# A language-model layer on one core: Down tail on 128 rows, quantiser in two list steps, four sums on GpSimd, new lists

## What is computed

```python
emb = (w0[inputs] @ w1) * mask * 16.0                     # A: rows of 512, then 512 x 256
x = layernorm(emb)                                         # y, the residual of the block
h = layer_norm(x, ln1_g, ln1_b); hx = token_shift(h)
k, v, r = mixes of h and hx, each @ (256 x 256); r = sigmoid(r)
wkv = wkv_scan(k, v, time_decay, time_first)               # recurrence over time, per channel
x = x + (r * wkv) @ wo                                     # B
h = layer_norm(x, ln2_g, ln2_b); hx = token_shift(h)
kk = square(relu(mix(h, hx) @ cwk)); rr = sigmoid(mix(h, hx) @ cwr)
x = x + rr * (kk @ cwv)                                    # 256 -> 1024 -> 256
h1 = emb + x
xq = fp4(layernorm(h1))                                    # C
g = silu(xq @ fp4(w_gate).T) * (xq @ fp4(w_up).T)          # 256 -> 704
out = h1 + fp4(g) @ fp4(w_down).T                          # 704 -> 256
```

## Time and profile before

| | us |
|---|---|
| median of 3 runs | 775.6 (773.82 to 776.73) |
| span of the profiled execution | 772.5 |
| one period, 145.65 to 230.13 | 84.48 |
| PE busy over the span | 701.0 (91%) |
| DVE | 591.7 (77%) |
| ACT | 509.2 (66%) |
| POOL | 144.3 (19%) |
| mean granted TensorE clock | 0.964 |

### The profile page before, as it was taken

How to read it: one execution, slowest core, us unless ns; L and a number is a source line. 1 busy time by engine, 2 the same in 40 slices (tenths; PEclk the granted TensorE clock), 3 DMA queues, 4 the chain that set the end, 5 groups by cost and what they waited for, 6 DMA issues and landing times.

```text
span 772.5 us, 9862 instructions
## 1 busy us (share of the span) xinstructions
PE 701.0 (91%) x3301; PEld 563.6 (73%) x3301; DVE 591.7 (77%) x1023; ACT 509.2 (66%) x888; POOL 144.3 (19%) x220
## 2 busy tenths in 40 slices
PE   4465788899999999999999999999999999899676
PEld 3325656787788867886788777896888777788574
DVE  0678777888788879788778878887988878872763
ACT  2556796698568966597749866797749774861221
POOL 2403301430032302230142103230232003000000
PEclk9687899999999999999999999999999999899999
DMA  4800000000010000010010001000010000000000
GB/s 124 275 2 27 3 25 2 27 10 20 15 41 1 28 14 14 28 28 1 14 42 2 28 15 41 1 28 10 4 42 1 1 14 15 1 0 14 15 0 28
DMA packets 13374, 19.34 MB, mean 25 GB/s; under 512 B 982, under 2 KB 10764, under 8 KB 13324
## 3 DMA queue, kind: packets, MB, share of 16 engines
q1 hardware_dynamic: 10720, 10.31, 4.1%
q0 software_dynamic: 2560, 8.39, 3.7%
q10 hardware_dynamic: 44, 0.01, 0.0%
HBM read 14.51 MB, written 4.19 MB: 24 GB/s over the span
## 4 chain that ended last, share of the span: by engine, by line
PE 74%; DVE 11%; ACT 9%; issue 4%; DMA 1%; POOL 0%; ACTq 0%; DVEq 0%; POOLq 0%
PE psB L556 20%; PE psC L652 11%; PE psC L625 11%; PE psB L583 11%; PE psA L547 9%; PE psA L519 5%; PE psC L639 3%; PE psA L507 2%; ACT hT L745 1%; ACT mix L754 1%; DMA rows<-L_tok_w,ids_now 1%; DVE top L360 1%; ACT take L800 1%; PE psA L529 1%; PE psC L611 1%
## 5 line engine op out<-in xcount | busy, mean ns | idle before, releaser
L556 PE MATMUL psB<-cwv_s,kkT 128*128 128x256 f32 x512 | 113.9, 380 | 0.0
L556 PEld LDWEIGHTS psB<-cwv_s,kkT 128*128 128x128 f32 x512 | 96.2, 190 | 15.7 <-issue 3.3
L652 PE MATMUL psC<-downT,hqT 128*128 128x256 f32 (+1 forms) x384 | 96.7, 397 | 0.0
L625 PE MATMUL psC<-up_hi,xq_hi 128*128 128x352 f32 x256 | 88.2, 345 | 9.2 <-DVE xq_lo L1202 8.5
L547 PE MATMUL psA<-mix,kvr_s 128*128 128x512 f32 x192 | 88.6, 606 | 3.4 <-ACT vT L776 2.4
L652 PEld LDWEIGHTS psC<-downT,hqT 128*128 128x128 f32 (+1 forms) x384 | 69.4, 192 | 26.4 <-issue 19.0
L625 PE MATMUL psC<-up_hi,xq_lo 128*128 128x352 f32 x256 | 83.8, 327 | 0.0
L625 PE MATMUL psC<-up_lo,xq_hi 128*128 128x352 f32 x256 | 83.6, 327 | 0.0
L447 POOL TENSOR_SCALAR sc_c<-mv_c 128x2 f32<-128x2 f32 x16 | 7.0, 436 | 371.7 <-DVE mv_c L1134 371.7
L547 PEld LDWEIGHTS psA<-mix,kvr_s 128*128 128x128 f32 x192 | 36.5, 194 | 42.4 <-issue 39.3
L519 PE MATMUL psA<-w_s,rowsT 128*128 128x256 f32 x256 | 59.5, 386 | 0.0
(11 more groups left out here) (163 smaller groups left out, 1488.5 us busy)
## 6 DMA issues: line engine op xcount, KB each, us to landing
out<-h SPq DMA_DIRECT2D x16, 256.0 KB, 2.1
mix<-L_attn_cwk SPq DMA_DIRECT2D x1, 1024.0 KB, 8.0
cwv_s<-L_attn_cwv SPq DMA_DIRECT2D x1, 1024.0 KB, 10.9
kkT<-L_ffn_w_gate SPq DMA_DIRECT2D x1, 704.0 KB, 4.6
kkT<-L_ffn_w_up SPq DMA_DIRECT2D x1, 704.0 KB, 6.7
hqT<-L_ffn_w_down SPq DMA_DIRECT2D x1, 704.0 KB, 7.8
w_s<-L_tok_w SPq DMA_DIRECT2D x1, 512.0 KB, 3.9
rows<-L_tok_w,ids_now POOLq DMA_INDIRECT x32, 4.0
```

The lines of the kernel that those rows point to most:

```text
L556: mm = nc.tensor.matmul(psB[:, B.slot(name), q * D:(q + 1) * D], lhsT[:, k, (2 * j + q) * P:(2 * j + q + 1) * P], weight[:, k, :], start=( ...
L625: mm = nc.tensor.matmul(psC[:, C.slot(name), f, 0:INTER // 2], a[:, k, t * P:(t + 1) * P], b[:, w, k, f * (INTER // 2):(f + 1) * (INTER // ...
L652: mm = nc.tensor.matmul(psC[:, C.slot(name), 0, q * D:(q + 1) * D], hqT[0:n, q, k, :], downT[0:n, k, :], start=(k == 0), stop=(k == KI - 1))
```

## The change

Line numbers of the changed kernel differ from those of the profile.

1. **Tail on 128 rows.** `downT` and `hqT` get zeros once in rows 64 to 127 of their sixth piece (four ScalarE activations in `w_turn2`), and every Down matmul contracts 128 rows. The transposes of the tail stay at 64.
2. **Quantiser in two steps.** `scale_blocks` (4 operations) and `round_blocks` (3 operations) are steps of their own (`c_sn`, `c_rn` for the normalised pairs, `c_sq`, `c_rq` for the tiles), so other steps can stand between them; `square` and `scales` have two buffers.
3. **Four groups on GpSimd.** `newv` and `numer` (2 operations of 128 x 512 each), `b_low` (2) and the addition of `b_value0` and `b_value1` (`b_final0`, `b_final1`, 1 each): 8 operations for a chunk leave DVE.
4. **New lists** for every engine, some buffers moved (`y` lies in `takev`, the raw weights in `hq`).

```diff
+    "act": [... ("a_wkv1", -1), ("a_wkv2", -1), ("c_sq3", 1), ("a_v", -1), ("c_norm0", 0), ("a_wkv3", -1),
+        ("c_sqn0", 0), ("c_turn2", 1), ("a_r", -1), ("w_turn2", 0), ("c_norm1", 0), ("c_turn3", 1), ...],
+    "dve": [("b_value0", 3), ("c_rq2", 4), ("w_split1", 3), ("c_stat0", 3), ("c_rq3", 4), ("a_wkv2", 2),
+        ("a_wkv3", 2), ("b_value1", 3), ("c_sn0", 3), ("c_stat1", 3), ("c_down0", 4), ("a_wkv4", 2), ("c_rn0", 3), ...],
+    "pool": [("b_final0", 0), ("a_newv", -1), ("c_coef0", 0), ("gather0", -2), ("b_final1", 0), ("a_numer", -1),
+        ("c_coef1", 0), ("gather1", -2), ("b_sum", -1), ("b_coef", -1), ("b_low", -1), ("a_coef", -2)],
...
+            def newv_a(ch):
+                for d in range(H):
+                    at(pool, wkv_exp, ch, EXPS.index(f"new{d}") + 1)
+                    A.wait_emptied(pool, ch, f"v{d}")
+                    A.wait_full(pool, ch, "v1")
+                    nc.gpsimd.tensor_tensor(numer[:, d], e_new[:, d], vT[:, d], ALU.mult).then_inc(wkv_sums.sem, 1)
+
+            def numer_a(ch):
+                for d in range(H):
+                    at(pool, wkv, ch, WKV.index(f"sumv{d}") + 1)
+                    at(pool, wkv_sums, ch, WKV_SUMS.index(f"newv{d}") + 1)
+                    nc.gpsimd.tensor_tensor(numer[:, d], numer[:, d], takev[:, d, :, 0:T], ALU.add).then_inc(wkv_sums.sem, 1)
+
+            def low_b(ch):
+                for d in range(H):
+                    at(pool, b_high, ch, d + 1)
...
+                    nc.gpsimd.tensor_tensor(key_lo[:, d], mix2[:, 0, d].rearrange("p c t -> p (c t)"), key_hi[:, d].bitcast(F32),
+                                            ALU.subtract).then_inc(b_low.sem, 1)
+
+            def final_b(j):
+                def step(ch):
+                    at(pool, b_sum, ch, 1)
+                    B.wait_emptied(pool, ch, f"cv{j}")
+                    pair = slice(2 * j, 2 * j + 2)
+                    nc.gpsimd.tensor_tensor(h1[:, ch.parity, pair, :], h1[:, ch.parity, pair, :], rr[:, pair, :], ALU.add
+                                            ).then_inc(b_fin.sem, 1)
...
                         for k in range(KI):
-                            n = P if k < KI - 1 else TAIL
-                            mm = nc.tensor.matmul(psC[:, C.slot(name), 0, q * D:(q + 1) * D], hqT[0:n, q, k, :],
-                                                  downT[0:n, k, :], start=(k == 0), stop=(k == KI - 1))
+                            mm = nc.tensor.matmul(psC[:, C.slot(name), 0, q * D:(q + 1) * D], hqT[:, q, k, :],
+                                                  downT[:, k, :], start=(k == 0), stop=(k == KI - 1))
...
+                            nc.scalar.activation(downT[TAIL:P, KI - 1, d * P:(d + 1) * P], ident[TAIL:P, :], ACT.Copy, scale=0.0
+                                                 ).then_inc(s_wd, 1)
...
+            def scale_blocks(ch, n, data, nb):
+
+                big, scale = scales[:, n % 2, 0, 0:nb], scales[:, n % 2, 1, 0:nb]
+                done = SCALED * n
+                at(dve, rounded, ch if n >= 2 else ch.back(1), ROUNDED * ((n - 2) % (2 + TILES) + 1))
+                nc.vector.tensor_reduce(big, blocks(data), AX_X, ALU.max, apply_absolute_value=True).then_inc(scaled.sem, 1)
...
+            def round_blocks(ch, n, data, nb):
+
+                w, scale = square[:, n % 2, 0:nb * BLOCK].bitcast(F32), scales[:, n % 2, 1, 0:nb]
+                done = ROUNDED * n
+                at(dve, squared, ch, n + 1)
...
```

More of the change, by code:

```diff
@@ L165 @@
           ("hq2", "act"), ("hq3", "act"), ("d1", "dve")]
-WKV = ["pad"] + [f"{step}{d}" for step in ("top", "gain", "now", "takev", "sumv", "sum1", "newv", "numer", "denom",
-                                           "near", "fix", "avg", "att")
-                 for d in range(H)]
+WKV = ["pad", "padv"] + [f"{step}{d}" for step in ("top", "gain", "now", "takev", "sumv", "sum1", "denom", "near", "fix",
+                                                   "avg", "att")
+                         for d in range(H)]
+WKV_SUMS = [f"{step}{d}" for step in ("newv", "numer") for d in range(H)]
 EXPS = [f"{step}{d}" for step in ("rise", "fall", "keep", "take", "new", "log", "inv") for d in range(H)]
 QUANT = 7
+SCALED, ROUNDED = 4, 3
 MIX_A, MIX_B = ("mix_k", "mix_v", "mix_r"), ("cmix_k", "cmix_r")
@@ L735, in y_a @@
                 at(act, a_coef, ch, 7)
[L736 removed]
+                at(act, wkv_sums, ch, len(WKV_SUMS))
                 for t in range(TILES):
@@ L766, in project @@
             def project(name):
-                dst, last = {"k": (kT, "gain"), "v": (vT, "newv"), "r": (rT, None)}[name]
+                dst, last = {"k": (kT, "gain"), "v": (vT, "takev"), "r": (rT, None)}[name]
                 def step(ch):
@@ L1098, in mix_b @@
                 shifted_mix(ch, hT2, mix2, MIX_B, b_part, b_mixed)
-            def low_b(ch):
-                for d in range(H):
-                    at(dve, b_high, ch, d + 1)
-                    if d == 0:
-                        B.wait_full(dve, ch.back(1), "kk7")
-                    nc.vector.tensor_tensor(key_lo[:, d], mix2[:, 0, d].rearrange("p c t -> p (c t)"), key_hi[:, d].bitcast(F32),
-                                            ALU.subtract).then_inc(b_low.sem, 1)
             def key_w(_):
```

126 lines of the change are left out of this document (74 added, 52 removed), and 34 rows, old and new, of the table ORDER.

## The result

The changed kernel takes 797.2 us (796.25 to 798.62), the kernel before 775.0 in the runs beside it: ratio 1.0286, interval 1.0264 to 1.0309. It is 22 us slower where 7 us faster was forecast. The time stands near the second rival (GpSimd and VectorE exclude each other, 790.7), above the stated range.

What follows compares the result with a forecast made beforehand. TensorE's own work was taken to bound the period. Terms -12.6 - 2.8 + 12.6 + 1 - 5.5 = -7.3 took 772.5 to 765.2, plus 3.1 for the median: 768.3 us; 8-in-10 range 755 to 788.

Steps and rivals of the forecast that it cites:

- the second rival: In the periods, VectorE operations with two SBUF inputs wait for GpSimd sums: 5.0 us a period, 790.7 us; chance 0.27.
- What bounds the kernel: In a period of 84.48 us TensorE is busy 84.02; only less TensorE work or a new TensorE wait changes it.
- The tail (-12.6): Down steps: full rows save 0.79 us at each of 16 steps, all on TensorE's path, -12.6 us.
- The two present waits (-2.8): TensorE's waits of 0.24 and 0.22 us for the second split and ScalarE's copy go: -0.46 a period, six periods.
- GpSimd side late and VectorE not held: Sums moved to GpSimd: each waits for VectorE's current operation (1.18 us plus 0.69), while VectorE's next operation isn't delayed.
- the wait on ScalarE's copy of tile 3: Second half of the second Down: TensorE waits 1.3 us a period, the coefficients of pair 1 taking 3.15.
- The second tight place: The key: `a_coef` stands behind `b_high` and two `b_low` on GpSimd, a wait of 0.5 us a period.
- +12.6: New TensorE waits in the second Down (1.3 us) and at the key (0.5), over seven periods or parts of one.
- Filling (+1): Ahead of the periods: output projection no earlier, weight split and chunk 0's norm earlier; +1 us, between -4 and +4.
- the fourth rival: In the filling, chunk 0's path comes 6 us or more later and TensorE's clock falls: 775 us; chance 0.08.
- Draining (-5.5): Behind the periods: split of pair 1 earlier by 2.7 us, two late waits gone; -5.5 us, between 0 and -8.
- the first of the signs named as "wrong": VectorE operations of 128x704 or 128x512 longer than 0.9 and 0.7 us beside the moved sums would show mutual exclusion.

Runs made afterwards that it cites:

- v_all: The changed kernel with all four groups of sums back on VectorE, lists otherwise as changed: 780.3 us, ratio 1.0090.
- measuring kernel: Three separate kernels, computing nothing of the layer, that time VectorE forms beside GpSimd sums; a two-SBUF-input sum went from 0.68 to 1.65 us.
- a_numer: The changed kernel with GpSimd's two `numer` sums behind the coefficients of pair 1 instead of ahead of them: 802.4 us, ratio 1.0362.

## Why the prediction was wrong

- **What bounds the kernel**: right. All that moved the time is waits of TensorE and the tail.
- **The tail (-12.6)**: right in kind, somewhat too large. The step is 5.18 us and the steady period 82.9, as said; alone it gives 9.5 us. The zero writes, which I had put at nothing, cost 0.8 of wait and, by the clock behind it, the 1.7 of the first period; the filling has 1.1 more, which stays open. Inside the changed kernel the tail is worth 7.5.
- **The two present waits (-2.8)**: they went, and waits of 0.46 and 0.28 came. The cut by itself gives 2.1, at the ends.
- **The failing step: "GpSimd side late and VectorE not held".** I took the end of the bound that the nearest rows showed, and those rows had no GpSimd operation long enough beside them. Each of the two engines is held by the other. In the stretch that I counted, the first Down's sum was due at 18.7 us without holds; it ends at 23.2 (384.74 to 407.89), and three holds of 0.95, 0.95 and 3.2 make the difference of 4.5 with 0.6 to spare. The path was wrong with it: the wait on ScalarE's copy of tile 3 behind late coefficients, 1.3 in the count, is absent, and TensorE waits 3.78 ahead of tile 3's transposes for VectorE, where I had it in time by 0.9 (18.7 against 19.6). The second tight place was nearly right (0.5 forecast, 0.74 measured). For +12.6 the traces have, in the six periods alone and against the kernel with the tail alone, 23.1 us of waits (25.9 less 2.8) and 7.8 of slower work (503.4 less 495.6). With the sums on VectorE the two are 14.8 and 4.8.
- **The clock had no term.** I held it to be full in the periods; behind the 3.78 it is 0.50 for over 3 us.
- **The rival's own price** was too low: 87.3 for a period (82.3 and 5.0) against 88.8. I had `b_final0` and one `newv` meet the rounding, which they do; I had nothing for the 3.2 us hold, as the scale operation has one input, and I didn't count one-input forms. The sum of its waits came near by luck: 1.5 at tile 3's transposes, 2.4 more until tile 3's copy and 1.1 at the key were counted, 3.78, none and 0.74 measured. The rest is the clock's 1.7. The stated range ended at 788, below the point of this rival, to which I had given 0.27.
- **Filling (+1)**: wrong; +10.2, of which the tail's kernel has 1.9, the lists 3.1 and GpSimd 5.2 (the three differences in the table). So the fourth rival, a filling of 6 us or more, came true beside the second. TensorE waits 4.8 us for the sigmoid of `r` and 2.6 for the recurrence there (4.5 and 1.4 in v_all):

```profile
143.41 1.94 PE L540 MATMUL psA<-ident,rows 128*128 128x128 f32 x8 [4.78 <-ACT rT L810]
147.91 1.62 PE L589 MATMUL psB<-wo_s,rT 128*128 128x256 f32 x3 [2.56 <-DVE rT L1036]
```

- **Draining (-5.5)**: with the four shorter Downs -8.7, measured -9.1.
- **What would show it**: the first of the signs named as "wrong", VectorE operations over 0.9 and 0.7 us beside the four groups, is what the trace shows, and so are the period over 86 and stage C's columns later than 148.

The Trainium skill (SBUF — State Buffer, "SBUF: two separate sides") names the forms that exclude each other: on VectorE's side those in a two-port mode or with two SBUF inputs. The measuring kernel agrees: 0.68 to 1.65 for two inputs, 0.42 to 1.38 for the `tensor_scalar`, none for the reduction. I had worked that rule out as a rival and given it 0.27.

Open: in the layer the scale operation is held to the end of three GpSimd sums (3.4 us; 1.1 with `b_final1` alone), while in the measuring kernels VectorE always got in after the first. Signals, in-place and strided operands don't make it there, each tried by itself; what does was not found, and the gathers that GpSimd issues just ahead of these sums were not tried. It is also not shown which ring sets the 88.8 us of a_numer.

## What to carry to other kernels

A sum moved from VectorE to GpSimd is only free where VectorE meanwhile reads PSUM, reduces or rests; elsewhere it can hold VectorE for nearly its own, longer, duration (1.2 us for 0.7), and the hold is counted as VectorE's busy time. A long duration is then neither work nor a wait by itself: compare it with the least of its form, with the granted clock, and with the engine's idle time in the period. When the trace of before has no row for one side of a bound, give that side the weight that it has, not that of the rows that happen to be there. In a kernel whose engines wait on each other in a ring, compare whole lists by the period: a wait taken away at one place came back in part at the next three times here.
